# A two-layer macaron block on one core: four weight buffers, four row buffers, three result buffers, and row loads issued ahead of weight loads

## The reference, cut to what matters

```
x = x + 0.5 * moe(layernorm(x))          # stage n = 0
x = x + attention(layernorm(x))          # stage n = 1, 16 heads
x = x + 0.5 * moe(layernorm(x))          # stage n = 2
x = x + 0.5 * fp4_ffn(layernorm(x))      # stage n = 3
x = x + retention(layernorm(x))
x = x + 0.5 * fp4_ffn(layernorm(x))
```

```
for e in range(8):
    h = silu(x @ w_gate[e].T) * (x @ w_up[e].T)        # 128 -> 256
    out = out + dense_w[:, e:e + 1] * (h @ w_down[e].T) # 256 -> 128
```

## Time and profile before

| | us |
|---|---|
| median of the runs shown (2268.72 and 2268.86) | 2268.79 |
| the profiled execution, its own time | 2260.8 |
| its span | 2259.0 |
| PE busy | 1542.7 (68%) |
| DVE busy | 1171.3 (52%) |
| ACT busy | 940.7 (42%) |
| mean DMA rate over the span | 51 GB/s |

### The profile page before, as it was taken

One profiled execution on the slowest core, in us unless ns is written; L12 is line 12 of the kernel. 1 busy time (PEld: TensorE's weight loads), 2 busy tenths in 40 slices (PEclk: granted clock), 3 DMA queues, 4 the chain that ended last, 5 costly groups with the idle time before them and its releaser, 6 DMA issues.

```text
span 2259.0 us, 25733 instructions
## 1 busy us (share of the span) xinstructions
PE 1542.7 (68%) x9017; PEld 837.3 (37%) x9017; DVE 1171.3 (52%) x1765; ACT 940.7 (42%) x1957; POOL 557.6 (25%) x966
## 2 busy tenths in 40 slices
PE   4345454555559999999999853454545467899777
PEld 3234343443111111111111232343434345666566
DVE  5200001111959999999999352111011139968896
ACT  1111111112158888888888721111111134566464
POOL 5720022125440000000000247100222026444411
PEclk9866666777569999999999975666666677999898
DMA  5221222222110101101001022212222210000001
GB/s 188 89 77 58 70 75 81 71 82 91 56 61 18 32 21 32 32 18 44 21 23 32 8 73 89 79 59 70 73 80 70 70 49 19 1 2 2 2 1 38
DMA packets 97457, 116.23 MB, mean 51 GB/s; under 512 B 14368, under 2 KB 76512, under 8 KB 97104
## 3 DMA queue, kind: packets, MB, share of 16 engines
q1 hardware_dynamic: 89136, 97.78, 14.6%
q0 software_dynamic: 8192, 16.79, 2.4%
HBM read 82.28 MB, written 35.26 MB: 52 GB/s over the span
## 4 chain that ended last, share of the span: by engine, by line
PE 52%; DMA 12%; DVE 11%; issue 7%; POOL 6%; ACT 6%; SPq 5%; POOLq 0%; ACTq 0%; DVEq 0%
PE PS L569 13%; DMA slots_in<-slots_x 11%; PE PS L1030 11%; PE PS L1018 8%; PE PS L581 4%; PE PS L1007 4%; DVE neg_half L1165 3%; PE PS L558 3%; ACT probs L1106 2%; POOL slots_x L472 2%; SPq L512 2%; PE PS L1715 2%; SPq L514 2%; ACT slots_out L636 2%; SPq L531 1%
## 5 line engine op out<-in xcount | busy, mean ns | idle before, releaser
L1165 DVE TENSOR_REDUCE neg_half<-PS 128x2 f32<-128x1024 f32 x512 | 601.4, 1220 | 73.2 <-PE PS L1007 58.1
L1106 ACT ACTIVATE probs<-PS 128x512 f32<-128x512 f32 x1024 | 528.8, 603 | 110.8 <-PE PS L1018 109.8
L711 DVE TENSOR_TENSOR shared<-shared,PS 128x512 f32<-128x512 f32 x92 | 63.3, 688 | 830.8 <-PE PS L569 740.4
L558 PE MATMUL PS<-ident,slots_in 128*128 128x128 f32 x184 | 61.4, 436 | 466.9 <-DMA slots_in<-slots_x 444.4
L569 PE MATMUL PS<-slotsT,w_ring 128*128 128x256 f32 x736 | 322.2, 616 | 0.0
L1018 PE MATMUL PS<-qk_all 51*128 51x512 bf16 x1024 | 278.5, 386 | 23.6 <-ACT probs L1106 17.9
L1030 PE MATMUL PS<-probs,Vg 128*32 128x512 f32 x2048 | 273.6, 606 | 0.1
L569 PEld LDWEIGHTS PS<-slotsT,w_ring 128*128 128x128 f32 x736 | 228.9, 326 | 47.5
L623 ACT ACTIVATE slotsT<-PS 128x256 f32<-128x256 f32 x92 | 35.3, 384 | 495.3 <-PE PS L558 471.8
L487 POOL DMA_INDIRECT came<-slots_y,place x128 | 127.9, 999 | 460.6 <-DMA slots_y<-slots_out 423.1
L1007 PE MATMUL PS<-qk_all 48*128 48x512 bf16 x1024 | 199.4, 400 | 42.6 <-DVE neg_half L1165 25.5
(11 more groups left out here) (217 smaller groups left out, 1949.2 us busy)
## 6 DMA issues: line engine op xcount, KB each, us to landing
w_ring<-in_w_experts SPq DMA_DIRECT2D x92, 384.0 KB, 3.1
slots_in<-slots_x SPq DMA_DIRECT2D x92, 128.0 KB, 3.0
slots_y<-slots_out SPq DMA_DIRECT2D x92, 128.0 KB, 1.8
split<-qk_all SPq DMA_DIRECT2D x16, 384.0 KB, 3.3
qk_all<-split SPq DMA_DIRECT2D x64, 96.0 KB
qk_all<-split SPq DMA_DIRECT2D x64, 64.0 KB
slots_x<-tokens_all,place POOLq DMA_INDIRECT x128, 2.2
came<-slots_y,place POOLq DMA_INDIRECT x128, 2.6
```

What stands on the lines that cost most here:

```text
L558: last = pe.transpose(bank(0)[:, j * P:(j + 1) * P], slots_in[:, k % RING_TILES, j, :], ident[:, :])
L1106: act.activation(probs[:, n % 2, STRIPS * strip + pair, :], bank(RING_AT + use % RING), ACT.Exp, scale=ATT_SCALE).then_inc(s["exped"], 1)
L1165: dve.tensor_reduce(neg_half[m % 2][:, i % 2, :, at], bank(use_bank(i, m), 2).rearrange("p (s w) -> p s w", s=STRIPS), AX.X, ALU.max, nega ...
```

## The change

Each ring gets its own length: four buffers of weights, four of rows, three of results. SP loads three tiles of weights and four tiles of rows before its loop. In turn i it issues the rows of tile i + 4, then the weights of tile i + 3, then waits for and stores tile i. A buffer is waited for as before, by the ring's own length: the rows of tile i + 4 wait for `turned(i)`, the weights of tile i + 3 for `down(i - 1)`. PE, ACT, DVE and POOL keep their programs and orders; only buffer numbers and semaphore names follow the new lengths.

```diff
-RING_TILES = 3
+W_RING, IN_RING, OUT_RING = 4, 4, 3
...
-        w_ring = sb("w_ring", [P, RING_TILES, EXPERT_WORDS])
-        slots_in = sb("slots_in", [P, RING_TILES, SLOTS_TILE // P, C])
+        w_ring = sb("w_ring", [P, W_RING, EXPERT_WORDS])
+        slots_in = sb("slots_in", [P, IN_RING, SLOTS_TILE // P, C])
...
-            part, r = i // PART_TILES, k % RING_TILES
+            part, r = i // PART_TILES, k % W_RING
...
-            wait(sp, moe["y_ps"], k - RING_TILES + 1)
+            wait(sp, moe["y_ps"], k - W_RING + 1)
...
-            part, r = i // PART_TILES, k % RING_TILES
+            part, r = i // PART_TILES, k % IN_RING
...
-            wait(sp, moe["in_ps"], k - RING_TILES + 1)
+            wait(sp, moe["in_ps"], k - IN_RING + 1)
...
         def moe_sp(sp, n, at_tile=None, between=None):
-            AHEAD = RING_TILES - 1
-            for i in range(AHEAD):
+            for i in range(W_RING - 1):
                 moe_load_weights(sp, n, i)
             if between is not None:
                 between()
-            for i in range(AHEAD):
+            for i in range(IN_RING):
                 moe_load_slots(sp, n, i)
             for i in range(STAGE_TILES):
-                if i + AHEAD < STAGE_TILES:
-                    moe_load_weights(sp, n, i + AHEAD)
-                    moe_load_slots(sp, n, i + AHEAD)
+                if i + IN_RING < STAGE_TILES:
+                    moe_load_slots(sp, n, i + IN_RING)
+                if i + W_RING - 1 < STAGE_TILES:
+                    moe_load_weights(sp, n, i + W_RING - 1)
                 moe_store_slots(sp, n, i)
...
-                pe.wait_ge(s[f"in{k % RING_TILES}"], 16 * (k // RING_TILES + 1))
+                pe.wait_ge(s[f"in{k % IN_RING}"], 16 * (k // IN_RING + 1))
...
-                pe.wait_ge(s[f"w{k % RING_TILES}"], 16 * (k // RING_TILES + 1))
+                pe.wait_ge(s[f"w{k % W_RING}"], 16 * (k // W_RING + 1))
```

More of the change, by code:

```diff
@@ L106, in macaron @@
         rank = sb("rank", [P, TILES, EXPERTS])
-        w_ring = sb("w_ring", [P, RING_TILES, EXPERT_WORDS])
-        slots_in = sb("slots_in", [P, RING_TILES, SLOTS_TILE // P, C])
+        w_ring = sb("w_ring", [P, W_RING, EXPERT_WORDS])
+        slots_in = sb("slots_in", [P, IN_RING, SLOTS_TILE // P, C])
         slotsT = sb("slotsT", [P, 2, SLOTS_TILE])
-        slots_out = sb("slots_out", [P, RING_TILES, SLOTS_TILE])
+        slots_out = sb("slots_out", [P, OUT_RING, SLOTS_TILE])
         came = sb("came", [P, 2, GT, 2, C])
@@ L233, in macaron @@
         moe = stage_sems(ctx, nc, "moe", "xn xT_ps xT logit_ps logits shifted exped weighed members counts experts place scattered0 scattered1 "
-                         "w0 w1 w2 in0 in1 in2 out0 out1 out2 in_ps inT gu silu0 silu h y_ps y came0 came1 half_added x_acc")
+                         "w0 w1 w2 w3 in0 in1 in2 in3 out0 out1 out2 in_ps inT gu silu0 silu h y_ps y came0 came1 half_added x_acc")
         att = stage_sems(ctx, nc, "att", "xn xT_ps xTf q_ps k_ps qkf_half v_ps v_raw qkf rest1 part2 parts V to_dram0 to_dram1 strips filled read neg_step "
@@ L339, in uses_of @@
         def uses_of(k, slot):
-            return (k - slot + RING_TILES - 1) // RING_TILES
+            return (k - slot + OUT_RING - 1) // OUT_RING
         def moe_tokens(dve, n, g):
@@ L481, in moe_gather @@
                 end = tile_of(n, (part + 1) * PART_TILES)
-                for r in range(RING_TILES):
+                for r in range(OUT_RING):
                     pool.wait_ge(moe[f"out{r}"], 16 * uses_of(end, r))
@@ L527, in moe_store_slots @@
             k = tile_of(n, i)
-            part, r = i // PART_TILES, k % RING_TILES
+            part, r = i // PART_TILES, k % OUT_RING
             sp.wait_ge(moe["y"], k + 1)
@@ L554, in turned @@
                 k = tile_of(n, i)
-                pe.wait_ge(s[f"in{k % RING_TILES}"], 16 * (k // RING_TILES + 1))
+                pe.wait_ge(s[f"in{k % IN_RING}"], 16 * (k // IN_RING + 1))
                 wait(pe, s["inT"], k)
                 for j in range(SLOTS_TILE // P):
-                    last = pe.transpose(bank(0)[:, j * P:(j + 1) * P], slots_in[:, k % RING_TILES, j, :], ident[:, :])
+                    last = pe.transpose(bank(0)[:, j * P:(j + 1) * P], slots_in[:, k % IN_RING, j, :], ident[:, :])
                 last.then_inc(s["in_ps"], 1)
@@ L562, in gate_up @@
                 k = tile_of(n, i)
-                w = w_ring[:, k % RING_TILES, :]
+                w = w_ring[:, k % W_RING, :]
                 pe.wait_ge(s["inT"], k + 1)
-                pe.wait_ge(s[f"w{k % RING_TILES}"], 16 * (k // RING_TILES + 1))
+                pe.wait_ge(s[f"w{k % W_RING}"], 16 * (k // W_RING + 1))
                 wait(pe, s["h"], k - 1)
@@ L634, in result @@
                 act.wait_ge(s["y_ps"], k + 1)
-                wait(act, s[f"out{k % RING_TILES}"], 16 * (k // RING_TILES))
-                act.activation(slots_out[:, k % RING_TILES, :], bank(1)[:, 0:SLOTS_TILE], ACT.Copy
+                wait(act, s[f"out{k % OUT_RING}"], 16 * (k // OUT_RING))
+                act.activation(slots_out[:, k % OUT_RING, :], bank(1)[:, 0:SLOTS_TILE], ACT.Copy
                                ).then_inc(s["y"], 1)
```

## The result

The changed kernel takes 1684.99 us, median of 2 runs (1683.97 to 1686.02), against 2268.79: a ratio of 0.7427, 95% interval 0.7395 to 0.7459. Forecast were 1677 us and a range of 1650 to 1750. Five later runs of the same kernel, in the experiments, gave a median of 1683.19.

The account below looks back on a forecast made before the run. PE was held in a 10.14 us turn, waiting 4.9 us for rows issued behind the previous store. 2260.8 - 316 (stage n = 2) - 276 (stage n = 0) = 1669 us, with 8 for the median 1677; range 1650 to 1750.

Parts of the forecast that it names:

- The ring: Tile loop: rows issued behind the previous tile's store make PE wait 4.9 us per 10.14 us turn; rows four ahead remove it.
- PE's own turn: Tile loop: without the pause, PE at full clock sets a turn of 2.89 us; 74 in 100.
- The rival in which the clock falls: Tile loop: PE's short stops keep the clock low, a turn of 5.67 us, 256 us more, 1933; 10 in 100.
- The ground for the full clock: Every tile turn was to have full clock because attention, with PE busy 622.88 of 660 us, showed 0.98.
- The weights: Next late load in the tile loop: landing 3.1 us after issue, they were to hide with 0.8 us to spare.
- SP's part: SP's queue per turn: weights start about 1.57 us after the store, which starts 0.45 us after `down(i - 1)`.
- their rival: Weights come late in the tile loop: landing 5.1 us, a turn of 3.5 us, 56 us more, 1733; 12 in 100.
- two rivals' prices: Late weights: landing 5.1 us, 56 us more, 12 in 100. Queue backing up: landing 18 us, 2269 us, 2 in 100.
- Stage n = 0: Tiles plus attention preparation: 220.4 + 18.7 + 23 puts the last projection at 262 instead of 538.14; gain 276 us.
- The waits for `prep_second`: Stage n = 0: ACT waits for POOL and so holds up PE twice, 9 and about 8 us.
- Stage n = 2: 46 turns of 2.89 us, stage some 138 us long, ending at about 1521 instead of 1837.05; gain 316 us.
- The 8 us for the median: Added to the profiled sum of 1669 because the earlier runs' median stood 8 us above the profiled execution; gives 1677.

Follow-up runs that it names:

- experiment 2: The changed kernel with three row buffers instead of four, rows loaded three tiles ahead; 1716.26 us.
- experiment 3: The kernel before with only the weights' part of the change: four weight buffers, three ahead; rows still two ahead, behind the weights; 2259.59 us.
- experiment 1: The changed kernel with three weight buffers instead of four, weights two tiles ahead, rows still four ahead; 1799.33 us.
- experiment 6: The changed kernel with a fifth weight buffer, weights loaded four tiles ahead; 1675.23 us.
- experiment 7: The changed kernel with ACT's `prep_second` two turns later in stage n = 0, behind the next group's `prep_evacuate`; 1661.99 us.
- experiment 4: The kernel before with 18 unused identity matmuls added behind each `down` in stage n = 2, filling PE's pause; 2179.07 us.
- experiment 8: The changed kernel with both a fifth weight buffer and the later `prep_second`; 1649.46 us.

## Why the prediction was right, point by point

**The ring, right.** The rows' wait went (line 558), and experiments 2 and 3 show that the rows' lead did it: with two tiles it was there, with three most of it was gone, with four all of it. What their place ahead of the weights did is not shown apart from that.

**PE's own turn, right, a little long.** 2.89 us was forecast for a turn without a wait; it is 2.84. The clock is 1.00 in both stages, as was taken from the attention. The rival in which the clock falls did not come about. The rule of the Trainium skill that was named for it (page "TensorE: Matmul & The Clock Gate", section "A second HAM failure mode: psum-queue depth-cycling", by which frequent short stops send the clock to and fro) does not show here: a dozen stops of up to 0.8 us in the two stages left 1.00. The longer stops of experiment 1, at 0.86, are waits for a load, which that section sets apart.

The ground for the full clock was weaker than it looked. The prediction took it from a stretch in which PE is as steadily busy; but in the last part of the attention, in the profile of after, PE was as busy at the low level:

```profile
1036.00:1044.00 8.00, 7.36 (x28) 1.24 (x26) 1.73 (x2) 4.62 (x9) 2.03 (x2) 0.50 0.00 0
```

So a busy share of 92% did not tell the clock there: that the tiles would have the full one came true, but did not follow from the attention stretch.

**The weights, the term that was mis-sized.** They were to hide with 0.8 us to spare at a landing of 3.1 us, and a share of 0.75 to 0.92 on the DMA engines was named as the unknown. The share came out at 0.81 to 0.85, and the landing, over all 92 loads, at 3.8, 4.5 at most. SP's part was right. First the landing, then three rows of SP's queue in stage n = 0 (start, us, line, operation):

```profile
DMA to landing us min/median/max: 2.9/3.8/4.5
...
104.42 0.36 SPq L531 DMA_DIRECT2D slots_y<-slots_out  x1
104.83 0.46 SPq L523 DMA_DIRECT2D slots_in<-slots_x  x1
106.08 0.36 SPq L514 DMA_DIRECT2D w_ring<-in_w_experts  x1
```

The weights start 1.66 us after the store; 1.57 was forecast. The formula for the bound was not quite right: it counted two turns from `down(i - 1)` to `gate_up(i + 3)`, but a turn in which the weights are late still does its 2.8 us of gate, up and down behind the wait. Three turns hold 0.45 + 1.66 + landing + 2.8: at 3.1 us that is 2.67 a turn, at 3.8 it is 2.90, and at 4.5 it is 3.14. PE's own turn is 2.84, so from the median landing on the weights bind as much as PE does. The mean turn shows it: 3.01 us over the last 46 of stage n = 2 ((1261.45 - 1122.90) / 46). So the late weights came, as a mild form of their rival: experiment 6 puts their price at 8.0 us. The same correction touches two rivals' prices: a landing of 5.1 us would make a turn of 3.3 us and not 3.5, 39 us and not 56, and to bring back a turn of 10.14 the weights would have had to land after more than 25 us and not after 18.

**Stage n = 0, right as a sum.** Forecast was the projection at 262; it came at 264.3. The waits for `prep_second` were to be 9 and 8 us and were 9.70 and 9.67, the 0.96 that was counted elsewhere included: 17.5 beside 17. ACT's rows in their stretch have the cause that was named, line 868 waiting for POOL; below them, what POOL's `ln_finish` waited for (us in total, times, longest):

```profile
215.93 1.06 ACT L868 ACTIVATE qk_all<-probs 128x1024 bf16<-128x1024 f32 x1 [9.92 <-POOL probs L880]
243.68 1.06 ACT L868 ACTIVATE qk_all<-probs 128x1024 bf16<-128x1024 f32 x1 [9.90 <-POOL probs L880]
...
POOL ln_a L297 <- DVE stats L279: 18.3, 2, 17.9
```

The parts of the sum can be read off: ACT waits 9.92 us, PE gets 2.85 us further before it stops, and starts again 2.63 us after ACT's release: 9.92 - 2.85 + 2.63 = 9.70, and nearly the same the second time. That the first wait would be longer because POOL still gathers did not show: POOL had been waiting for DVE's statistics for 0.4 us by then.

Two errors cancel in part: the turns up to 188 us had a mean of 3.05 rather than 2.89 ((188.48 - 87.67) / 33), and the low clock behind the two waits cost about 2 us each time (line 829 at 2.07 rather than 1.13, and line 830 as much) where 3 was taken. POOL's side of the reason, that the wait would stay because its cause is DVE's add and POOL's own work behind it and not a load, held; experiment 7 shows that the order on ACT decides whether PE sees it.

**Stage n = 2, 5.7 us over.** Forecast 138, measured 143.7: the 46 turns at 3.01 instead of 2.89 make 5.5 of the difference. DVE's adds hid nearly, as was said: line 581 is idle for 0.7 us in all.

**The 8 us for the median, right for a reason that wasn't known.** The sum was 1669 for the profiled execution, and 8 were added because the runs of before stood that much above their profile. The stages were 2.3 + 5.7 = 8 over the forecast; from 1669 that makes 1677, and the profiled execution took 1686.0. The other 9 us lie outside the change. The last part of the attention, from its last row-max combine to the first tile of stage n = 2, took 132.4 us in the profile of before (1250.8 to 1383.2) and 141.1 in that of after (976.7 to 1117.8), with the same instructions in the same order. Busy time of its first 75 us, before and after:

```profile
1250.80:1325.80 75.00, 56.60 (x366) 22.13 (x366) 24.77 (x77) 47.16 (x92) 21.18 (x66) 0.98 0.05 8
```

```profile
976.70:1051.70 75.00, 63.28 (x355) 22.29 (x354) 22.51 (x74) 46.38 (x91) 21.23 (x66) 0.84 0.04 6
```

The clock is 0.98 in one and 0.84 in the other. But this is not the change's doing: experiments 3 and 4, which have the old pause, took 140.7 and 140.6 us over this stretch, all other profiles but experiment 1's (135.1) 140.4 to 141.3. The profiled execution of before was the exception. That its other runs, 2262.7 to 2271.3, have the long stretch is likely and not shown, since none of them was profiled; the mean granted clock of nine of them, 0.811 to 0.813 against 0.815 in the profiled one, goes with it. If so, the "8 above the profile" were the price of this stretch in both kernels, and that the forecast came within 8 us of the median owes as much to luck as to the sum.

**Two slips that changed nothing.** The upper end of the forecast's own range is 1677 + 23 + 15 = 1715, not 1717. And between the use of the rows and that of the weights stands, beside a `turned` and a `gate_up`, also a `down`.

## What to carry to other kernels

A lead is enough when the turns that it spans are at least as long as three things together: the time from the end of a `down` to the issue of the load behind it, the landing, and the work that still follows the wait for it, up to the end of that turn's `down`. Weights loaded three tiles ahead span three turns here, rows loaded four ahead three as well. Reckon with the landing that the faster loop will have, not with that of now: here it grew from 3.1 to 3.8 us. In a ring, ask first which of its loads the bound engine asks for soonest behind its issue: here the fourth weight buffer alone gave some 5 us, and the rows' lead without it left 114. When a pause goes that covered other engines' waits, look in their queues for work that stands ahead of what the bound engine needs: moving it was worth 21 us, more than the next buffer.

## What the runs showed of the hardware

The median landing of the 384 KB load was longer in kernels that kept the DMA engines busier, although the loads of one turn start apart: 3.1 us at a share of 0.21, 3.3 at 0.51 to 0.59 (experiment 1), 3.5 at 0.69 to 0.73 (experiment 2), 3.8 at 0.81 to 0.85, 4.1 at 0.83 to 0.90 (experiment 6). The shares are those of a long stretch in each of the two stages, the landings those of all 92 loads. No run varied the share alone, and it does not settle the landing: experiment 7 has 4.1 at 0.84.

The granted clock can differ between executions of the same instructions. In the first 75 us of the attention's last part it was 0.98 in the profile of before, 0.84 in that of after and 0.85 in the second one of the changed kernel, and the whole part was 132.4, 141.1 and 140.4 us long. Between executions of one program it differed as a mean over the run: 0.915 to 0.925 in experiment 8. Two rows of the same eight matmuls, before and after:

```profile
1300.94 1.07 PE L1030 MATMUL PS<-probs,Vg 128*32 128x512 f32 x8
```

```profile
1027.73 1.93 PE L1030 MATMUL PS<-probs,Vg 128*32 128x512 f32 x8
```

What decides between the two isn't settled: no run here changed that stretch.
